# Late tiles transposed by DMA, W loads on GpSimd's queue, and new engine orders in a fused quantized attention and LoRA kernel

## The chip, the cores and the metric

One core of one Trainium2 chip runs the kernel. The metric is the device time of one execution in microseconds (us); the time of a version is the median of several runs.

## The reference, cut to what matters

```python
h   = x + tanh(g_xattn) * (q(layernorm(x)) @ q(ctx))        # q: round(x / s + z), clipped to 0..255, minus z, times s
y   = layernorm(h)
top = argmax(y @ gate_w.T + expert_bias)                    # one of 4 experts for each row
out = h + tanh(g_ffn) * (y @ W_up.T + lora_B[top] @ (lora_A[top] @ y))
```

`x` is 2 x 1024 x 2048 and each batch has its own `ctx` of 2048 x 2048; `W_up` is 2048 x 2048; the LoRA rank is 8. Everything comes and goes as float32.

## The kernel before, in words

The 2048 rows of x are 16 tiles of 128 rows (TILES); tiles 0 to 7 belong to the first batch. There are two stages, and TensorE goes from the one into the other.

**Stage 1** computes h. For each tile, VectorE takes the moments of the row (`moments`, L590 to L594), ScalarE a square root (`sqrt`, L374), VectorE the scale (`quant_scale`, L607), ScalarE rounds to int16 (`quant`, L380) and VectorE clips to bf16 (`clip`, L642). The clipped tile `q1` lies in `halves`, which has room for two tiles. TensorE transposes it in 16 blocks of 128 x 128 (`transposes`, L951 to L960) into two PSUM banks, and ScalarE copies them out to `rows_T` (`evac`, L399; for tiles 0 to 3 VectorE takes the second half, L654). `rows_T` holds four transposed tiles. Then come four chunks of 512 columns, 16 matmuls each (`part`, L969 to L988). VectorE adds each chunk to the row tile (`epi`, L649), and GpSimd's queue stores tiles 0 to 11 of h to HBM (L339) and loads the row tiles 6 to 15 of x (L335). The last four tiles of h stay in SBUF. Each chunk needs four of the 32 context tiles, which SP loads (L258), ScalarE rounds (`ctx_round`, L407) and VectorE clips (`ctx_clip`, L659). The four first tiles run interleaved, since the context arrives while they run: `stage1` (L993 to L1030) has that order written out. From tile 4 on the order is tile by tile, and the transposes of tile t+1 stand behind the first chunk of tile t.

**W** is 16 tiles of 128 x 2084 (`in_w`), brought in over three buffers: `normed`, `stage0` and `stage1`. SP issues all of them (`load_w`, L260 to L276). Loads 0 to 7 are W tiles 0 to 7, each taken through `abs_sum` (ScalarE, L416), `w_pow` (VectorE, L667 to L673), `w_high` (ScalarE, L425) and `w_low` (VectorE, L679); the buffer is free after `w_low`. Tiles 8 to 15 can't be stored before the second batch's context is done with, so they are loaded twice: loads 8 to 15 are for `abs_sum` alone, and loads 16 to 23 for `w_high` and `w_low`. Load i waits for the buffer's former user, and load 18 for `y_low(0)` as well. The common scale comes from `scales` on VectorE and an all-reduce on GpSimd (L359).

**Stage 2** computes y in two halves (high and low, f16) and multiplies by both halves of W in three products. `norm`, `y_high` and `y_low` (L633, L438, L687) make y; the first two tiles are transposed by TensorE (`y_transposes`, L1043) and scaled by VectorE (`yT_out`, L699), the others by one DMA transpose each from SP (L312). The first tile of stage 2 runs over the W tiles in order, five column blocks for each, for W tiles 0 to 10 (L1112 to L1119), and waits at each for `s_lo`, the count of `w_low`. It then waits for all 16 W tiles (L1121) and does the rest. Fifteen tiles of 240 matmuls each follow.

The orders of ScalarE (L463 to L547) and VectorE (L784 to L938) are written out by hand: `period(p, a, b, c)` interleaves the work of one tile with W or context work. An engine does its list strictly in order, and so does a DMA queue: a wait holds up all that stands behind it.

## Time and profile before

| what | value |
|---|---|
| median of 3 runs | 966.54 us (965.98 to 968.11) |
| the profiled execution's own time | 966.78 us |
| its span in the trace | 965.0 us |
| TensorE busy | 936.3 us, 97% |
| VectorE, ScalarE, GpSimd busy | 473.9, 233.8, 16.7 us |
| chain that ended last, TensorE's share | 93% |
| HBM read and written | 90.38 and 29.37 MB |

Times in the trace count from the first instruction. In the rows, PE is TensorE, DVE VectorE, ACT ScalarE, POOL GpSimd, and SP the engine that only issues DMAs. A matmul's length in a row includes its filling and draining; the pace is what the start times and the chain show.

### The profile page before, as it was taken

The page shows a single profiled execution, that of the slowest core. Times are in us where ns is not written, and L with a number is a line of the kernel's source. Part 1 is how long each engine was busy: PE and PEld are TensorE (multiplying, and loading weights), DVE is VectorE, ACT ScalarE, POOL GpSimd, SP SyncE. Part 2 cuts the span into 40 slices and gives each one's busy share as a digit, 9 for nine tenths or more (in the row PEclk, how much of TensorE's full clock was granted, in tenths as well). Part 3 has the DMA queues.
Part 4 walks back from the last instruction along what each step waited for, and adds up shares of the span by engine and source line. Part 5 has one row for each costly group of instructions (what it writes and reads, how often), then busy time and mean ns, then how long its engine had stood idle before and what let it go on. Part 6 is the DMA issues. An engine that isn't in the chain of part 4 may idle for free.

```text
span 965.0 us, 12440 instructions
## 1 busy us (share of the span) xinstructions
PE 936.3 (97%) x5239; PEld 500.9 (52%) x5264; DVE 473.9 (49%) x1023; ACT 233.8 (24%) x195; POOL 16.7 (2%) x40
## 2 busy tenths in 40 slices
PE   2899999999998999999999999999999999999998
PEld 1444444444455555555555555555555555555554
DVE  6695757785857526153443516253443516253421
ACT  5886777677622100000000000000000000000000
POOL 0001100010000000000000000000000000000000
PEclk9999999999999999999999999999999999999999
DMA  8999977678562232322222232222222132121211
GB/s 344 420 376 398 422 275 295 222 285 293 205 179 88 88 88 74 102 44 88 44 88 44 88 94 76 93 44 88 44 88 64 70 85 44 44 44 44 44 44 44
DMA packets 77082, 135.27 MB, mean 140 GB/s; under 512 B 61936, under 2 KB 62080, under 8 KB 62720
## 3 DMA queue, kind: packets, MB, share of 16 engines
q1 hardware_dynamic: 71088, 92.74, 29.4%
...
HBM read 90.38 MB, written 29.37 MB: 124 GB/s over the span
## 4 chain that ended last, share of the span: by engine, by line
PE 93%; DVE 3%; DMA 2%; ACT 1%; issue 1%; SPq 0%; ACTq 0%; DVEq 0%
PE bank L1051 67%; PE bank L981 23%; PE bank L958 2%; PE bank L1060 1%; DVE arena L679 1%; DMA normed<-in_w 1%; DMA rows<-in_x 1%; DVE bn L590 1%; ACT arena L425 0%; PE bank L1043 0%; ACT arena L407 0%; DVE halves L642 0%; DVE arena L659 0%; DVE normed L633 0%; SPq L280 0%
## 5 line engine op out<-in xcount | busy, mean ns | idle before, releaser
L1051 PE MATMUL bank<-arena,rows_T 128*128 128x416 f16 (+1 forms) x3840 | 685.2, 339 | 2.5 <-DVE arena L679 2.5
L1051 PEld LDWEIGHTS bank<-arena,rows_T 128*128 128x128 f16 x3840 | 373.0, 97 | 308.1 <-issue 4.8
L981 PE MATMUL bank<-arena,rows_T 128*128 128x512 bf16 x999 | 224.0, 382 | 4.5 <-DVE arena L659 2.7
L981 PEld LDWEIGHTS bank<-arena,rows_T 128*128 128x128 bf16 x1024 | 99.8, 98 | 122.1 <-issue 4.5
L773 DVE SCALAR_TENSOR_TENSOR rows<-bank,derived,rows 128x416 f32<-128x416 f32 (+2 forms) x80 | 49.9, 641 | 213.9 <-PE bank L1051 213.9
L446 ACT ACTIVATE z_stack_T<-bank 96x128 f16<-96x128 f16 x16 | 4.4, 272 | 556.0 <-PE bank L1066 556.0
L590 DVE BATCH_NORM_STATS2 bn<-rows 128x6 f32<-128x512 f32 x124 | 76.6, 679 | 3.7 <-DMA rows<-in_x 3.6
L713 DVE SCALAR_TENSOR_TENSOR route<-bank,derived,scal 128x4 f32<-128x4 f32 x16 | 3.5, 221 | 109.1 <-PE bank L1051 109.0
L649 DVE SCALAR_TENSOR_TENSOR rows<-bank,derived,rows 128x512 f32<-128x512 f32 x60 | 44.7, 748 | 22.6 <-PE bank L981 22.0
L781 DVE SCALAR_TENSOR_TENSOR rows<-bank,z_back_scale,rows 128x512 f32<-128x512 f32 x64 | 45.1, 746 | 10.6 <-PE bank L1060 6.6
L689 DVE SCALAR_TENSOR_TENSOR halves<-normed,ln,halves 128x2048 f16<-128x2048 f32 x14 | 32.9, 2351 | 29.0 <-ACT halves L440 29.0
L407 ACT ACTIVATE arena<-arena,scal,derived 128x2048 int16<-128x2048 f32 x22 | 44.9, 2083 | 0.8 <-DMA arena<-in_ctx 0.8
L440 ACT ACTIVATE halves<-normed,ln 128x2048 f16<-128x2048 f32 x14 | 28.0, 2002 | 48.3 <-DVE normed L637 48.3
L958 PE MATMUL bank<-ident_bf,halves 128*128 128x128 bf16 x256 | 18.7, 230 | 18.1 <-DVE halves L642 17.6
L380 ACT ACTIVATE halves<-rows,ln 128x2048 int16<-128x2048 f32 x15 | 31.4, 2091 | 9.0 <-DVE ln L614 9.0
L637 DVE SCALAR_TENSOR_TENSOR normed<-rows,ln,stage 128x2048 f32<-128x2048 f32 x14 | 32.9, 2352 | 0.5
L659 DVE TENSOR_SCALAR arena<-arena,derived 128x2048 bf16<-128x2048 int16 x32 | 23.8, 749 | 15.2 <-ACT arena L407 15.1
L679 DVE SCALAR_TENSOR_TENSOR arena<-stage,wscale,arena 128x2084 f16<-128x2084 f32 x11 | 26.1, 2383 | 9.9 <-ACT arena L425 9.8
L958 PEld LDWEIGHTS bank<-ident_bf,halves 128*128 128x128 bf16 x256 | 16.9, 104 | 22.5 <-issue 16.7
L399 ACT ACTIVATE rows_T<-bank 128x1024 bf16<-128x1024 bf16 x28 | 27.1, 1013 | 5.2 <-PE bank L958 5.2
L425 ACT ACTIVATE arena<-stage,wscale 128x2084 f16<-128x2084 f32 x11 | 22.1, 2027 | 22.4 <-DMA stage<-in_w 13.0
L599 DVE RECIPROCAL ln<-ln 128x1 f32<-128x1 f32 x32 | 5.1, 159 | 33.2 <-ACT ln L374 33.2
...
## 6 DMA issues: line engine op xcount, KB each, us to landing
arena<-in_ctx SPq DMA_DIRECT2D x22, 1024.0 KB, 15.7
stage<-in_w SPq DMA_DIRECT2D x17, 1042.0 KB, 5.5
out<-rows ACTq DMA_DIRECT2D x15, 1024.0 KB, 3.9
h_scratch<-rows POOLq DMA_DIRECT2D x11, 1024.0 KB, 7.6
rows<-h_scratch SPq DMA_DIRECT2D x11, 1024.0 KB, 4.8
stage<-in_ctx SPq DMA_DIRECT2D x10, 1024.0 KB, 8.5
rows<-in_x POOLq DMA_DIRECT2D x10, 1024.0 KB, 8.6
normed<-in_w SPq DMA_DIRECT2D x7, 1042.0 KB, 7.4
```

Of the source, the lines that this page charges most:

```text
L380: A(q1_i16(t), Xt(t), ACT.Relu, bias=L(t, "qb"), scale=L(t, "qs")).then_inc(s_qi, 1)
L407: A(Qc(c, True), buf, ACT.Relu, bias=z2, scale=V["rs2"]).then_inc(s_cr, 1)
L590: v.bn_stats(bn[:, u % 2, i, :], Xc(u, i * 512, (i + 1) * 512)).then_inc(s_bn, 1)
L637: v.scalar_tensor_tensor(out=T[:, 0:D], in0=Xt(u), scalar=L(u, "mean"), in1=WR, op0=ALU.subtract, op1=ALU.mult).then_inc(s_norm, 1)
L649: v.scalar_tensor_tensor(out=xs, in0=bank[ROT[g % 6]][:, :], scalar=V["coef"], in1=xs, op0=ALU.mult, op1=ALU.add).then_inc(s_epi, 1)
L679: v.scalar_tensor_tensor(out=W(n, 1), in0=wbuf[k][:, :], scalar=wa[:, n:n + 1], in1=W(n, 0), op0=ALU.mult, op1=ALU.subtract).then_inc(s_lo, 1)
L689: v.scalar_tensor_tensor(out=HL[:, 1, :], in0=T[:, 0:D], scalar=L(TILES + s, "rstd"), in1=HL[:, 0, :], op0=ALU.mult, op1=ALU.subtract).the ...
L773: v.scalar_tensor_tensor(out=xs, in0=bank[c][:, a - CUT[c]:b - CUT[c]], scalar=V["gs"], in1=xs, op0=ALU.mult, op1=ALU.add).then_inc(s_e2, 1)
L781: v.scalar_tensor_tensor(out=xs, in0=TR[j % 2], scalar=gl[:, s % 2:s % 2 + 1], in1=xs, op0=ALU.mult, op1=ALU.add).then_inc(s_el, 1)
L958: mm = nc.tensor.transpose(TR[g].bitcast(BF16)[:, i * P:(i + 1) * P], q1(t)[:, k * P:(k + 1) * P], idb[:, :])
L981: mm = mmul(bk, q1T[:, t % 4, kt, :], Q(b, n, kt), start=(kt == 0), stop=(kt == KT - 1 and not slow), skip_group_check=True)
L1051: mm = mmul(bank[c][:, 0:b - a], YT[:, s % 2, yh, kt, :], W(kt, wh, a, b), start=(first and kt == kts[0] and yh == 0 and wh == 0), stop=(k ...
```

## The change

Tiles 9 to 15 of `q1` are transposed by DMA from SP into `rows_T` (`q1_transpose`) instead of by TensorE and ScalarE; two semaphores, for even and odd tiles, count them, and `by_dma` waits for them. SP also gets the row tiles 11 to 15, the stores of tiles 7 to 11, the load of `b_t` and the small LoRA loads. All 24 W loads go to GpSimd's queue, behind its last row load and store, with the all-reduce between loads 17 and 18. From tile 8 on ScalarE and VectorE have a new order, written out item by item; around the start of stage 2, `w_low(9)` to `w_low(11)` stand earlier. At the start of the kernel the orders of all engines change too: row tile 2 is loaded ahead of context tile 1, tiles 1 and 2 are rounded and transposed earlier, and TensorE gets 6 and 8 products of zeros (384 columns each, on the zeroed `d1`, into a bank that is overwritten) around the transposes of tile 0. The diff is without the semaphores' declarations and the context lines; the body of `load_w` is as at L260 to L276, with pool for sp.

```diff
+    BY_DMA = 9
+    BY_SP = 7
...
+    BY_V = [(1, 0), (2, 1), (3, 1)]
...
-by_pool = [u for u in range(SPARE + 1, TILES)] + [TILES + KEEP]
+by_pool = [u for u in range(SPARE + 1, BY_SP + 4)]
...
-        return s_hg[slot(u)], count(u, range(TILES - KEEP))
+        if u < BY_SP:
+            return s_hg[slot(u)], count(u, range(BY_SP))
+        return s_h[slot(u)], count(u, range(BY_SP, TILES - KEEP))
...
+def by_dma(engine, t):
+    engine.wait_ge(s_xt[t % 2], 16 * ((t - BY_DMA) // 2 + 1))
...
-        if u >= TILES:
+        if u > SPARE:
...
-    def load_w(i):
...
+    def q1_transpose(t):
+        sp.wait_ge(s_q1, t + 1)
+        sp.wait_ge(s_mm, place[(t - 4, NCH - 1)] + 1)
+        sp.dma_start_transpose(q1T[:, t % 4], q1(t)).then_inc(s_xt[t % 2], 16)
+    def store(t):
+        sp.wait_ge(s_epi, place[(t, NCH - 1)] + 1)
+        sp.dma_start(h_t[t], Xt(t)).then_inc(s_h[slot(t)], 16)
...
+    row(2)
...
-    row(2)
-    for c in range(2, 6):
-        ctx_tile(c)
+    ctx_tile(2)
+    ctx_tile(3)
...
+    ctx_tile(4)
+    ctx_tile(5)
...
-    for i in range(KT + 8):
-        load_w(i)
+    row(11)
+    store(7)
+    q1_transpose(9)
+    row(12)
+    q1_transpose(10)
+    q1_transpose(11)
+    store(8)
+    row(13)
+    store(9)
+    q1_transpose(12)
+    row(14)
+    store(10)
+    q1_transpose(13)
+    store(11)
+    row(15)
+    q1_transpose(14)
+    q1_transpose(15)
+    sp.wait_ge(*stored(former(TILES + KEEP)))
+    sp.dma_start(Braw, b_t).then_inc(s_braw, 16)
...
+    sp.wait_ge(s_bp, 2)
+    sp.dma_start(brow_d, bp[0:E * R, 1:2]).then_inc(s_br0, 16)
+    sp.wait_ge(s_br0, 16)
+    sp.dma_start(br[:, :], brow_d.rearrange("k o -> (k o)").unsqueeze(0).to_broadcast(
+        [P, E * R])).then_inc(s_br, 16)
...
+    sp.wait_ge(s_bst, 1)
+    row(TILES + KEEP)
...
+    nc.gpsimd.memset(d1[:, :, :], 0.0).then_inc(s_pool, 1)
...
-    pool.wait_ge(s_pool, 2)
+    pool.wait_ge(s_pool, 3)
...
-    nc.gpsimd.memset(d1[:, :, :], 0.0).then_inc(s_id, 1)
...
-        if u >= TILES:
-            pool.wait_ge(*stored(u - TILES - KEEP))
-            src = h_t[u - TILES - KEEP]
-        else:
-            src = x_t[u]
-        nc.gpsimd.dma_start(Xt(u), src).then_inc(s_xg[slot(u)], 16)
+        nc.gpsimd.dma_start(Xt(u), x_t[u]).then_inc(s_xg[slot(u)], 16)
...
-    for t in range(7, TILES - KEEP):
-        store(t)
-        row(t + 4)
-    pool.wait_ge(*stored(former(TILES + KEEP)))
-    nc.gpsimd.dma_start(Braw, b_t).then_inc(s_braw, 16)
+    def load_w(i):
+        n, k = W_LOADS[i]
...
+        if i == KT + 2:
+            pool.wait_ge(s_yl, 1)
+        nc.gpsimd.dma_start(wbuf[k][:, :], w_t[n]).then_inc(s_w[k], 16)
+    for i in range(KT + 2):
+        load_w(i)
...
-    pool.wait_ge(s_bp, 2)
-    nc.gpsimd.dma_start(brow_d, bp[0:E * R, 1:2]).then_inc(s_br0, 16)
-    pool.wait_ge(s_br0, 16)
-    nc.gpsimd.dma_start(br[:, :], brow_d.rearrange("k o -> (k o)").unsqueeze(0).to_broadcast(
-        [P, E * R])).then_inc(s_br, 16)
-    pool.wait_ge(s_bst, 1)
-    row(TILES + KEEP)
+    for i in range(KT + 2, KT + 8):
+        load_w(i)
...
-        if t >= 2:
+        if t >= BY_DMA + 2:
+            by_dma(act, t - 2)
+        elif t >= 2:
...
-            if t >= 1:
+            if t > BY_DMA:
+                by_dma(act, t - 1)
+            elif t >= 1:
...
+    def half(t, g):
+        act.wait_ge(s_tr, 2 * t + g + 1)
+        if t >= 4:
+            act.wait_ge(s_mm, place[(t - 4, NCH - 1)] + 1)
+        A(q1T[:, t % 4, GROUP * g:GROUP * (g + 1), :].rearrange("p k m -> p (k m)"),
+          TR[g].bitcast(BF16), ACT.Copy).then_inc(s_ev, 1)
...
-        for g in range(1 if t < HEAD else 2):
-            act.wait_ge(s_tr, 2 * t + g + 1)
-            if t >= 4:
-                act.wait_ge(s_mm, place[(t - 4, NCH - 1)] + 1)
-            A(q1T[:, t % 4, GROUP * g:GROUP * (g + 1), :].rearrange("p k m -> p (k m)"),
-              TR[g].bitcast(BF16), ACT.Copy).then_inc(s_ev, 1)
+        half(t, 0)
+        half(t, 1)
...
-            act.wait_ge(s_tr, 2 * TILES)
+            by_dma(act, TILES - 2)
+            by_dma(act, TILES - 1)
...
+    sqrt(1)
...
-    sqrt(1)
-    evac(0)
+    half(0, 0)
+    quant(1)
+    half(0, 1)
+    sqrt(2)
...
-    quant(1)
+    quant(2)
+    half(1, 1)
...
-    sqrt(2)
-    evac(1)
-    quant(2)
+    half(2, 0)
...
-    evac(2)
+    sqrt(3)
...
-    sqrt(3)
+    quant(3)
...
-    quant(3)
...
-    evac(3)
+    half(3, 0)
...
-        evac(p + 1)
+        if p + 1 < BY_DMA:
+            evac(p + 1)
...
-    period(8, lambda: abs_sum(0), lambda: w_high(0), lambda: abs_sum(1))
-    for p in range(9, 12):
-        n = 2 * p - 17
-        period(p, lambda: (w_high(n), abs_sum(n + 1)), lambda: w_high(n + 1), lambda: abs_sum(n + 2))
-    period(12, lambda: (w_high(7), abs_sum(8)), lambda: abs_sum(9), lambda: abs_sum(10))
-    period(13, lambda: abs_sum(11), lambda: abs_sum(12), lambda: abs_sum(13))
-    period(14, lambda: abs_sum(14), lambda: (sqrt(TILES), abs_sum(15)), lambda: y_high(0))
+    abs_sum(0)
+    sqrt(10)
+    w_high(0)
+    abs_sum(1)
+    quant(10)
+    abs_sum(2)
+    w_high(1)
+    sqrt(11)
+    quant(11)
+    sqrt(12)
+    abs_sum(3)
+    w_high(2)
+    abs_sum(4)
+    quant(12)
+    w_high(3)
+    abs_sum(5)
+    w_high(4)
+    w_high(5)
+    abs_sum(6)
+    sqrt(13)
+    w_high(6)
+    quant(13)
+    abs_sum(7)
+    w_high(7)
+    sqrt(14)
+    abs_sum(8)
+    abs_sum(9)
+    quant(14)
+    abs_sum(10)
+    sqrt(15)
+    abs_sum(11)
+    quant(15)
+    abs_sum(12)
+    abs_sum(13)
+    abs_sum(14)
+    sqrt(16)
+    abs_sum(15)
+    y_high(0)
...
-    for n in range(8, 14):
+    for n in range(8, KT - 1):
...
-    for n in range(14, KT):
-        w_high(n)
+    w_high(KT - 1)
...
-        dve.wait_ge(s_id, 2 + E)
+        dve.wait_ge(s_pool, 3)
+        dve.wait_ge(s_id, 1 + E)
...
-    def moments(u):
+    def moments(u, first=0, end=4):
...
-        for i in range(4):
+        for i in range(first, end):
...
-            elif i == 3 or u > 0:
+            elif i in (3, first):
...
+        if end < 4:
+            return
...
-    def evac_second(t):
-        dve.wait_ge(s_tr, 2 * t + 2)
-        v.tensor_copy(q1T[:, t % 4, GROUP:2 * GROUP, :].rearrange("p k m -> p (k m)"),
-                      TR[1].bitcast(BF16)).then_inc(s_evb, 1)
+    def half(t, g):
+        dve.wait_ge(s_tr, 2 * t + g + 1)
+        v.tensor_copy(q1T[:, t % 4, GROUP * g:GROUP * (g + 1), :].rearrange("p k m -> p (k m)"),
+                      TR[g].bitcast(BF16)).then_inc(s_tv, 1)
...
+    def scalars():
+        dve.wait_ge(s_tanh, 2)
+        step(v.tensor_tensor(V["coef"], s1, s2, ALU.mult))
+        step(v.tensor_tensor(V["coef"], V["coef"], V["tx"], ALU.mult))
+        step(v.tensor_scalar(V["cd"], V["coef"], V["dl2"], -1.0, ALU.mult, ALU.mult))
+        step(v.tensor_scalar(V["ce"], V["cd"], V["dl1"], -float(D), ALU.mult, ALU.mult))
...
+    scalars()
...
-    dve.wait_ge(s_tanh, 2)
-    step(v.tensor_tensor(V["coef"], s1, s2, ALU.mult))
-    step(v.tensor_tensor(V["coef"], V["coef"], V["tx"], ALU.mult))
-    step(v.tensor_scalar(V["cd"], V["coef"], V["dl2"], -1.0, ALU.mult, ALU.mult))
-    step(v.tensor_scalar(V["ce"], V["cd"], V["dl1"], -float(D), ALU.mult, ALU.mult))
...
-    ctx_clip(0)
...
-    evac_second(0)
-    ctx_clip(1)
...
+    quant_scale(2)
+    ctx_clip(0)
+    ctx_clip(1)
+    clip(2)
+    half(1, 0)
+    moments(3, 0, 2)
...
-    quant_scale(2)
-    evac_second(1)
-    clip(2)
+    half(2, 1)
...
-    evac_second(2)
+    moments(3, 2, 4)
+    quant_scale(3)
...
-    moments(3)
...
+    ctx_clip(6)
+    clip(3)
...
-    quant_scale(3)
-    ctx_clip(6)
+    ctx_clip(7)
+    delta_parts()
...
-    ctx_clip(7)
+    ctx_clip(8)
...
-    clip(3)
-    evac_second(3)
+    half(3, 1)
...
+    ctx_clip(9)
...
+    ctx_clip(10)
...
-    ctx_clip(8)
-    ctx_clip(9)
-    ctx_clip(10)
-    delta_parts()
...
-    period(8, lambda: w_pow(0), nothing, lambda: (w_low(0), w_pow(1)))
-    for p in range(9, 12):
-        n = 2 * p - 17
-        period(p, lambda: w_low(n - 1) if n > 1 else None, lambda: (w_low(n), w_pow(n + 1)), lambda: w_pow(n + 2))
-    period(12, lambda: w_low(6), lambda: w_low(7), nothing)
-    period(13, nothing, nothing, nothing)
...
-    period(14, lambda: moments(TILES), lambda: norm(0), scales)
+    epi(7, 3)
+    moments(10)
+    w_pow(0)
+    quant_scale(10)
+    w_low(0)
+    w_pow(1)
+    clip(10)
+    moments(11)
+    quant_scale(11)
+    epi(8, 0)
+    w_low(1)
+    clip(11)
+    epi(8, 1)
+    moments(12)
+    w_pow(2)
+    epi(8, 2)
+    epi(8, 3)
+    epi(9, 0)
+    w_pow(3)
+    epi(9, 1)
+    quant_scale(12)
+    epi(9, 2)
+    w_low(2)
+    w_low(3)
+    clip(12)
+    epi(9, 3)
+    epi(10, 0)
+    epi(10, 1)
+    w_pow(4)
+    epi(10, 2)
+    w_pow(5)
+    moments(13)
+    w_low(4)
+    epi(10, 3)
+    w_low(5)
+    epi(11, 0)
+    w_pow(6)
+    quant_scale(13)
+    epi(11, 1)
+    w_low(6)
+    epi(11, 2)
+    clip(13)
+    epi(11, 3)
+    epi(12, 0)
+    moments(14)
+    w_pow(7)
+    w_low(7)
+    epi(12, 1)
+    epi(12, 2)
+    quant_scale(14)
+    clip(14)
+    moments(15)
+    epi(12, 3)
+    quant_scale(15)
+    epi(13, 0)
+    epi(13, 1)
+    epi(13, 2)
+    clip(15)
+    epi(13, 3)
+    moments(16)
+    epi(14, 0)
+    norm(0)
+    epi(14, 1)
+    epi(14, 2)
+    scales()
...
+    w_low(9)
...
+    epi(15, 3)
+    w_low(10)
+    w_low(11)
...
-    epi(15, 3)
...
-    for n in range(9, 14):
-        w_low(n)
+    w_low(12)
+    w_low(13)
...
-        if g and t < HEAD:
-            pe.wait_ge(s_evb, t + 1)
+        if t >= BY_DMA:
+            by_dma(pe, t)
+        elif (t, g) in BY_V:
+            pe.wait_ge(s_tv, BY_V.index((t, g)) + 1)
...
-            pe.wait_ge(s_ev, t + 1 if t < HEAD else HEAD + 2 * (t - HEAD) + g + 1)
+            pe.wait_ge(s_ev, 2 * t + g + 1 - sum(1 for h in BY_V if h < (t, g)))
+    def zeros(n):
+        for i in range(n):
+            mmul(bank[0][:, 0:3 * P], d1[:, 0, :], d1[:, :, :].rearrange("p a b -> p (a b)"), start=True,
+                 stop=True)
...
+        pe.wait_ge(s_pool, 1)
+        pe.wait_ge(s_ve, 1)
+        zeros(6)
...
+        zeros(8)
+        transposes(1)
...
-        transposes(1)
+        transposes(2)
...
-        transposes(2)
+        part(0, 0, 3, 4, slow)
...
-        for t in range(LEAD):
-            part(t, 0, 3, 4, slow)
-        for k in range(3):
-            for t in range(LEAD):
-                part(t, 1, k, k + 1, slow)
-        transposes(LEAD)
-        for t in range(LEAD):
-            part(t, 1, 3, 4, slow)
+        part(2, 1, 0, 1, slow)
+        part(1, 0, 3, 4, slow)
+        part(2, 1, 1, 2, slow)
+        part(1, 1, 0, 1, slow)
+        part(0, 1, 0, 1, slow)
+        part(0, 1, 1, 2, slow)
+        part(2, 1, 2, 3, slow)
+        part(2, 0, 3, 4, slow)
+        part(1, 1, 1, 2, slow)
+        transposes(3)
+        part(1, 1, 2, 3, slow)
+        part(0, 1, 2, 3, slow)
+        part(0, 1, 3, 4, slow)
+        part(1, 1, 3, 4, slow)
+        part(2, 1, 3, 4, slow)
...
-                if n == 0 and t + 1 < TILES:
+                if n == 0 and t + 1 < BY_DMA:
...
-            half_out(TILES - 1, g)
+            half_out(BY_DMA - 1, g)
```

## Rows read from the trace of the kernel before

**Rows 1.** The page: busy time, share of the span and instructions of each engine

```profile
PE 936.3 (97%) x5239; PEld 500.9 (52%) x5264; DVE 473.9 (49%) x1023; ACT 233.8 (24%) x195; POOL 16.7 (2%) x40
```

**Rows 2.** TensorE in order of time, 0 to 120 us: start, length, instructions

```profile
16.04 0.80 PE L958 MATMUL bank<-ident_bf,halves 128*128 128x128 bf16 x6 [16.04 <-DVE halves L642]
...
25.12 1.89 PE L958 MATMUL bank<-ident_bf,halves 128*128 128x128 bf16 x16 [1.58 <-DVE halves L642]
...
34.35 12.90 PE L981 MATMUL bank<-arena,rows_T 128*128 128x512 bf16 x58 [1.40 <-DVE arena L659]
```

**Rows 3.** The chain that ended last, in order of time: start, length, what

```profile
207.27 0.89 PE bank L958 x16
...
221.98 0.89 PE bank L958 x16
...
292.79 2.39 DVE arena L679
...
303.33 5.29 PE bank L1051 x30
```

**Rows 4.** TensorE in order of time, 215 to 330 us

```profile
254.68 1.50 PE L1043 MATMUL bank<-ident_h,halves 128*128 128x128 f16 x24
...
263.54 29.25 PE L1051 MATMUL bank<-arena,rows_T 128*128 128x416 f16 x165
295.32 7.12 PE L1051 MATMUL bank<-arena,rows_T 128*128 128x416 f16 x30 [2.53 <-DVE arena L679]
```

**Rows 5.** Windows, TensorE alone: stretch, length, busy (instructions), granted clock, DMA share, GB/s

```profile
296.00:297.00 1.00, 1.00 (x5) 0.50 0.85 287
```

**Rows 6.** ScalarE in order of time, 0 to 320 us

```profile
17.75 1.02 ACT L399 ACTIVATE rows_T<-bank 128x1024 bf16<-128x1024 bf16 x1 [1.84 <-PE bank L958]
...
215.74 2.09 ACT L380 ACTIVATE halves<-rows,ln 128x2048 int16<-128x2048 f32 x1 [1.79 <-DVE ln L614]
...
275.75 2.03 ACT L425 ACTIVATE arena<-stage,wscale 128x2084 f16<-128x2084 f32 x1 [10.94 <-DMA stage<-in_w]
```

**Rows 7.** VectorE in order of time, 130 to 330 us

```profile
160.63 2.46 DVE L590 BATCH_NORM_STATS2 bn<-rows 128x6 f32<-128x512 f32 x4
...
208.65 2.46 DVE L590 BATCH_NORM_STATS2 bn<-rows 128x6 f32<-128x512 f32 x4
...
218.58 0.75 DVE L642 TENSOR_SCALAR halves<-halves,derived 128x2048 bf16<-128x2048 int16 x1
...
251.57 2.28 DVE L687 TENSOR_TENSOR halves<-normed,halves 128x2048 f16<-128x2048 f32 x1
...
265.10 2.38 DVE L679 SCALAR_TENSOR_TENSOR arena<-stage,wscale,arena 128x2084 f16<-128x2084 f32 x1
```

**Rows 8.** DMA issues, 130 to 250 us: engine, count, size, us to landing

```profile
stage<-in_w SPq DMA_DIRECT2D x13, 1042.0 KB, 5.5
h_scratch<-rows POOLq DMA_DIRECT2D x6, 1024.0 KB, 5.8
```

**Rows 9.** VectorE in order of time, 0 to 130 us

```profile
11.38 2.47 DVE L590 BATCH_NORM_STATS2 bn<-rows 128x6 f32<-128x512 f32 x4 [0.58 <-DMA rows<-in_x]
...
15.14 0.75 DVE L642 TENSOR_SCALAR halves<-halves,derived 128x2048 bf16<-128x2048 int16 x1
```

**Rows 10.** The instructions on rows_T that SP issues: DMA transposes

```profile
L312 SPq DMA_TRANSPOSE rows_T<-halves x14: 4731/4832/5502, 338.6 to 900.2; - x14
...
DMA to landing us min/median/max: 6.7/6.7/8.3
```

**Rows 11.** DMA queues, 338 to 347 us: packets, MB, share of the stretch

```profile
q1 hardware_dynamic: 4128, 1.05, 70.3%
```

**Rows 12.** DMA in 40 slices of 2 us, 160 to 240 us: GB/s

```profile
GB/s 208 370 426 381 197 63 333 138 4 393 266 398 416 167 333 150 0 393 250 422 413 167 325 154 0 393 279 398 438 304 243 388 408 408 434 400 292 271 0 38
```

**Rows 13.** Windows, all engines: busy, granted clock, DMA share, GB/s

```profile
189.09:203.79 14.70, 14.60 (x80) 7.17 (x80) 12.06 (x26) 10.61 (x11) 1.07 (x2) 1.00 0.71 268
```

**Rows 14.** What SP issues, in order of time, 0 to 420 us

```profile
142.60 0.80 SPq L276 DMA_DIRECT2D stage<-in_w  x2
```

More of the change, by code:

```diff
@@ L173, in build @@
         s_xg = [sem(f"row_tile_loaded_by_pool{i}") for i in range(XB)]
+        s_h = [sem(f"late_h_tile_stored{i}") for i in range(XB + 1)]
         s_hg = [sem(f"h_tile_stored{i}") for i in range(XB + 1)]
@@ L184, in build @@
         s_tr = sem("transposed"); s_ev = sem("transposes_out")
-        s_evb = sem("second_half_out")
+        s_tv = sem("transposes_out_by_vector")
         s_mm = sem("chunk_done"); s_epi = sem("chunk_out")
@@ L192, in build @@
         s_wc = sem("w_back_scale"); s_wr0 = sem("w_back_row_parked"); s_wr = sem("w_back_row_loaded")
-        s_dt = sem("y_transposed_by_dma")
+        s_xt = [sem(f"q1_transposed_by_dma{i}") for i in range(2)]; s_dt = sem("y_transposed_by_dma")
         s_m2 = sem("chunk2_done"); s_dl = sem("delta_done"); s_rt = sem("route_step"); s_zs = sem("z_stack_ready"); s_gl = sem("z_back_scale_ready")
@@ L352, in _ @@
             store(6)
[L353 to L357 removed]
+            def load_w(i):
+                n, k = W_LOADS[i]
+                before = [j for j in range(i) if W_LOADS[j][1] == k]
+                if not before:
+                    if k:
+                        pool.wait_ge(s_cr, CT)
+                    else:
+                        pool.wait_ge(*stored(SPARE))
+                if before:
+                    j = before[-1]
+                    if HALF <= j < KT:
+                        pool.wait_ge(s_sum, j + 1)
+                    else:
+                        pool.wait_ge(s_lo, j + 1 if j < HALF else j - HALF + 1)
+                if i == KT + 2:
[3 more added lines that the diff above has]
+                load_w(i)
             pool.wait_ge(s_pm, 1)
             nc.gpsimd.partition_all_reduce(V["PM"], V["pm"], P, bass.bass_isa.ReduceOp.max).then_inc(s_PM, 1)
[L360 to L366 removed]
+            for i in range(KT + 2, KT + 8):
+                load_w(i)
         @block.scalar
```

16 lines of the change are left out of this document (removed).

## The prediction

> **What bounds the kernel now.** I read the page first: TensorE is busy for 97% of the span [rows 1], so only work taken off TensorE, or a wait of it that ends earlier, can shorten the run. The chain of waits in order of time shows which. From 34.35 to 263.54 us it runs on TensorE without a wait: blocks of 16 transposes (L958, 0.89 us) and of matmuls, one block of transposes in each tile of 14.71 us (221.98 - 207.27) [rows 2 to 4]. VectorE and ScalarE lie beside it. TensorE loses time in two places. The first is the head: it starts at 16.04, and its matmuls have no wait left only from 34.35 on; 16 transposes there take 1.89 us in place of 0.89 [rows 2, 3], so TensorE ran at about half pace, the lower of its two levels (1.2 of 2.4 GHz). The second is the start of stage 2: 165 matmuls from 263.54, then a wait of 2.53 us for the last `w_low`, then 30 matmuls in 7.12 us where the same 30 later take 5.29; the granted clock is 0.50 in between [rows 3 to 5]. Stage 2 behind that is TensorE work that the change doesn't touch.
>
> **The change, part by part**, against the profiled execution (966.78 us, span 965.0; 0.24 above the median).
>
> **Transposes off TensorE.** Tiles 9 to 15 lose a block each: 7 x 0.89 = 6.2 us, all on the path [rows 3]. ScalarE loses 14 copies of about 1 us [rows 6], which were beside the path; they give it room.
>
> **Start of stage 2.** In the old list `w_low(9)` stands behind two epilogues, two `yT_out` and `b_scale`, and starts at 265.10 [rows 7]; load 20 (W tile 12) can be issued only when it ends, at 267.5, and its user on ScalarE starts at 275.75 after 10.94 us of waiting [rows 6]. In the new list `w_low(9)` goes ahead of about 4.3 us of that work, and 10 and 11 ahead of the two `yT_out`. Count from the first product of stage 2. `w_low(9)` ends near 0 (now +3.9), load 20 lands 5.5 later [rows 8]; `w_low(10)` and `(11)` end by +5.5; two `yT_out`, `b_scale` and `w_low(12)` take 2.4 + 0.6 + 2.4, to +10.9; load 23 lands at +16.4, and after `y_high(1)` (2.1), `w_high(15)` (2.0) and `w_low(15)` (2.4) all W is ready at about +23. TensorE asks for it at +29.3 (292.79 - 263.54) [rows 3, 4]. So the wait of 2.53 goes, and the low clock behind it (7.12 - 5.29 = 1.8): 4.4 us. With 6 us of slack even the late landing of now doesn't bring it back. Bounds: 0 and 4.4.
>
> **The W loads' queue.** In the same stretch a store from GpSimd lands 5.8 us after its issue and a W load from SP 5.5 [rows 8]. I take 0.3 us a load, hidden; bounds 0 and 1. Load 0 now waits behind `store(6)`, about 1 us, before the context is done, with no user yet. The all-reduce stands ahead of load 18, which waits for `y_low(0)` anyway. The small LoRA loads go to SP; `route(0)` needs them only after W is ready, 20 us after `b_scale`. These I cost at nothing.
>
> **Head.** `clip(0)` waits for the scalars behind `moments(1)`; ahead of them it starts some 0.8 us earlier, when `moments(1)` is through [rows 9]. The transposes of tile 1 start at 25.12 now. In the new list ScalarE does, from the moments' end at 14.3, `sqrt(1)` 0.2, `ctx_round(0)` 2.0, a copy 0.9 and `quant(1)` 2.0, VectorE a clip 0.7: 20.2. Up to 34.35 the old list did three blocks of transposes and 24 matmuls; from about 22 the new one has one block and these 24 left, 6.1 us at full clock. If the clock stays low until 30, as now, that ends near 32.2, which is 2.1 us of gain. Against it stands that context tiles come at their old pace, so part is waited away. I take 1.4; bounds 0 and 2.5. The products of zeros cost nothing while TensorE waits for `clip(0)` and `clip(1)`: 8 x 0.35 us at the low clock (384 columns, three times the 0.12 us of a transpose there, 1.89 / 16) end before 20.2. What they may do is raise the clock earlier. The Trainium skill (TensorE: Matmul & The Clock Gate, "What's actually happening") says that activity is what releases the throttle; by that the zeros might bring the upper bound, 2.5, in place of 1.4. The slow matmuls of the head and the 0.50 after the wait agree with it [rows 2, 5].
>
> **New waits of TensorE.** A DMA transpose of 1 MB occupies SP's issue for 4.8 us and lands after 6.7 [rows 10]; a tile of q1 is half of that: 2.4 us of all queues' time and 6.7 - 2.4 = 4.3 to landing when nothing is ahead. The upper bound is half the queues' share of that stretch, 0.703 x 9 / 2 = 3.2 us [rows 11]. It now needs a place among the W loads, at 2.5 us each (1.04 MB near 410 GB/s, what full slices move) [rows 12], and the DMA queues are already at 0.71 in such a tile [rows 13]. When TensorE wants a tile follows from the grid: a chunk takes (14.71 - 0.89) / 4 = 3.46 us, so after the block at 221.98 (tile 14's, behind the first chunk of tile 13) tile 14 begins at 221.98 + 0.89 + 3 x 3.46 = 233.2, tile 9 at 159.7 and tile 8 at 145.0. The tiles with the least room:
> - Tile 9 stands on SP behind `row(11)` and `store(7)`, which can go when tile 7 is done, 145.0 - 1.4 + 0.8 = 144.4. Loads 1 and 2, now at 142.60 [rows 14], come at the same time. Three transfers ahead: 144.4 + 7.5 + 4.3 = 156.2. TensorE wants it at 159.7 - 1.4 - 0.9 = 157.4. It holds, with 1.2 us to spare.
> - Tile 14: `quant(14)` is at 215.74 and its clip ends at 219.3 now [rows 6, 7]. TensorE wants it at 233.2 - 1.4 - 6 x 0.89 = 226.5. With one W load ahead it lands at 219.3 + 2.5 + 4.3 = 226.1, with two at 228.6. Loads 10 to 13 come together here, so I take two: 2.2 us.
> - `y_low(0)` ends at 253.85 and TensorE wants it at 254.68 [rows 4, 7]; now it is wanted 7.6 us earlier. It hangs on the W loads through `abs_sum(15)`. The new order is to speed this; I take 0.3.
> Together +2.5; bounds 0 (each lands in time) and 8.
>
> The sum: -6.2 - 4.4 - 1.4 + 2.5 = -9.5, so 966.78 - 9.5 = 957.3, and 957.0 on the scale of the median.
>
> **The rivals.**
> - *Transposes starve behind the W loads* (chance 0.15). 1.05 MB go in 4128 packets, some 254 bytes each [rows 11], and a row of W is 8.3 KB. If the two queues take turns packet by packet, a transpose gets almost nothing until GpSimd's queue is empty. Tile 14 then waits for all of loads 10 to 12, 219.3 + 7.5 + 4.3 = 231.1, 4.7 us late, and the low clock follows as after the 2.53 us of now (1.8): waits of 6.5 + 0.3 in place of 2.5, 961.3. For it speaks the packet size; against it, that no row shows the two together. The Trainium skill (DMA: Bandwidth & Descriptors, "Queues, rings and completion order") says that a DMA engine goes round its queues one packet at a time, though it counts several descriptors to a packet; the trace can't show here which it is.
> - *VectorE and the W work still set the pace* (0.12). From 160.63 to 208.65 the moments come every 16.0 us, not every 14.7: VectorE lags, and catches up only behind tile 13 [rows 7]. It is busy for 12.1 of 14.7 us there [rows 13], so the lag is waiting, not work. If the new order keeps it, `y_low(0)` is as late as 253.85 less the head's 1.4 and TensorE waits 5.4 us more: 962.4.
> - *The DMA queues fill up, and it gets slower* (0.09). Between 142.6 and 238 they must move W loads 1 to 17, five row tiles and five stores at 2.5 us each, `b_t` at 1.9, and seven transposes: 67.5 + 1.9 + 16.8 = 86 of 95 us. Let a transpose of 0.5 MB hold them as long as one of 1 MB does (4.8): 103 us. The overrun of 8 us comes once at tile 9, through late rows and W tiles, and again before `y_low(0)`, where now nothing is spare; with the clock's 1.8 each time, 12 to 16 us of waits against 12 of gain: 968. It decides from a price of about 4.5 us for a transpose (an overrun of 6 us, twice). Against it stands half the bytes and half the packets.
> - *The waits are nil and the head takes its upper bound* (0.12): 966.54 - 6.2 - 4.4 - 2.5 = 953.4.
>
> **How the numbers follow.** The forecast has 0.52. The range runs from 953.5 to 963.5: it holds the forecast, the first two rivals and most of the last. What a measurement of this kernel can tell from no change is about 0.2%, 1.9 us. Faster by more than that are all cases but the third rival, and a little of the second: 0.88. Within it 0.03, slower 0.09.
>
> **What would show it.** In the changed kernel: no L958-like blocks after tile 8 and a tile of 13.8 us; the transposes of tile 1 near 20; 165 matmuls at the start of stage 2 with no wait for W behind them and a clock of 1.00; and waits of TensorE for the transposes on `rows_T` at tile 14, some 2 us. The forecast is wrong if tile 9 waits too, or if the transposes land more than 10 us after their issue; then the DMA rivals hold.

## The result, and the profile after

| version | median | runs | ratio to before, 95% interval |
|---|---|---|---|
| before, run beside it | 965.91 us | 8 (963.98 to 968.11) | |
| after | 972.88 us | 8 (968.05 to 980.48) | 1.0079 [1.0051, 1.0108] |

The change makes the kernel slower, by 7 us, where 9.5 us of gain were forecast; the time lies outside the range. It also spreads more from run to run, over 12 us in place of 4. The profiled execution took 972.03 us.

The page of the kernel after: span, busy times, and two DMA queues (packets, MB, share of the span); q1 carries what SP issues, q0 what GpSimd issues.

```profile
span 970.0 us, 12227 instructions
...
PE 932.9 (96%) x5143; PEld 495.8 (51%) x5166; DVE 472.5 (49%) x1022; ACT 221.7 (23%) x182; POOL 23.3 (2%) x50
...
q1 hardware_dynamic: 84080, 83.14, 28.6%
q0 software_dynamic: 5184, 38.19, 11.9%
```

Against [rows 1], TensorE does less and the span is still 5.0 us longer. The waits of TensorE, in us, times and longest, say where it went:

```profile
PE bank L1130 <- DMA rows_T<-halves: 13.1, 2, 10.5
PE bank L1097 <- DVE derived L867: 11.6, 1, 11.6
PE bank L1107 <- DVE halves L720: 2.5, 2, 1.7
PE bank L1212 <- DVE arena L757: 2.4, 1, 2.4
```

L1097 and L1107 are the head. The first line is new: two waits, 13.1 us, for DMA transposes. The last is the old wait for the last `w_low` (L757, formerly L679), which was to go. TensorE in order of time shows both in place, 10 to 310 us:

```profile
20.53 1.89 PE L1107 MATMUL bank<-ident_bf,halves 128*128 128x128 bf16 x16 [0.72 <-DVE halves L720]
...
159.09 69.23 PE L1130 MATMUL bank<-arena,rows_T 128*128 128x512 bf16 x314 [2.65 <-DMA rows_T<-halves]
...
238.78 22.66 PE L1130 MATMUL bank<-arena,rows_T 128*128 128x512 bf16 x94 [10.46 <-DMA rows_T<-halves]
261.28 1.50 PE L1204 MATMUL bank<-ident_h,halves 128*128 128x128 f16 x24
...
270.14 29.25 PE L1212 MATMUL bank<-arena,rows_T 128*128 128x416 f16 x165
301.81 5.43 PE L1212 MATMUL bank<-arena,rows_T 128*128 128x416 f16 x30 [2.42 <-DVE arena L757]
```

The waits at 159.09 and 238.78 are for tiles 9 and 14. The 94 matmuls from 238.78 take 22.66 us; the same 94 take 20.88 in another run below, so the low clock after the wait (granted 0.50 from 239 to 242 us) costs 1.8. Stage 2 starts at 270.14, in place of 263.54 [rows 4]. The 30 matmuls at 301.81 have a wait of 2.42 ahead of them, nearly as before, but run in 5.43 and not in 7.12.

The chain that ended last, in order of time: start, length, what.

```profile
143.96 15.00 DMA rows_T<-halves
...
218.41 20.24 DMA rows_T<-halves
...
264.68 14.86 DMA stage<-in_w
...
289.54 7.60 DMA stage<-in_w
```

So a transpose of half a megabyte took 15.0 and 20.2 us from issue to landing, where one of a whole megabyte took 6.7 [rows 10], and a W load just before stage 2 took 14.9, where in stage 1 before they took 5.5 [rows 8] and at the start of stage 2 up to 10.0. The instructions on `rows_T` that SP issues, tiles 9 to 15 (duration in ns of the issue, minimum, median, maximum):

```profile
L275 SPq DMA_TRANSPOSE rows_T<-halves x7: 4727/7609/9526, 144.0 to 226.4; - x7
...
DMA to landing us min/median/max: 7.9/9.7/20.2
```

What the queues did is in the DMA view of three stretches (packets, MB, share of the stretch). From 218 to 222 us, with tile 14's transpose issued at 218.41:

```profile
DMA packets 216, 1.64 MB, mean 411 GB/s; under 512 B 19, under 2 KB 19, under 8 KB 19
...
q0 software_dynamic: 216, 1.64, 102.5%
```

from 222 to 226 us:

```profile
DMA packets 1884, 1.00 MB, mean 251 GB/s; under 512 B 1819, under 2 KB 1819, under 8 KB 1819
...
q0 software_dynamic: 81, 0.54, 126.7%
q1 hardware_dynamic: 1803, 0.46, 57.6%
```

and from 226 to 238 us:

```profile
DMA packets 1112, 2.17 MB, mean 181 GB/s; under 512 B 877, under 2 KB 877, under 8 KB 877
...
q1 hardware_dynamic: 846, 0.21, 48.1%
q0 software_dynamic: 266, 1.96, 39.9%
```

First GpSimd's queue has all of the engines, and the transpose gets nothing. Then 1803 of its packets go in 4 us; half of a whole megabyte's 4128 [rows 11] would be 2064, so little of tile 14 is left. But GpSimd has issued W loads at 220.88 and 223.69, SP issues tile 15's transpose at 226.41, and from 226 on everything crawls: 2.17 MB and 846 small packets in 12 us. W loads alone move 1.64 MB in 4, and transposes alone 4128 packets in 9 [rows 11]; at these two paces what went in the 12 us would have taken some 4.8 + 1.8 = 6.6 (an estimate). Tile 14 lands at 238.65, as the last of the two loads does.

### The profile page after: what moved, and what is told of

It reads as the page before. It is cut to its first block, busy times and chain, and to the rows that moved or that the text cites. A ratio compares the mean times of both kernels' runs of the same rounds, so it can differ in the third digit from the quotient of the medians.

```text
span 970.0 us, 12227 instructions
## 1 busy us (share of the span) xinstructions
PE 932.9 (96%) x5143; PEld 495.8 (51%) x5166; DVE 472.5 (49%) x1022; ACT 221.7 (23%) x182; POOL 23.3 (2%) x50
## 4 chain that ended last, share of the span: by engine, by line
PE 86%; DMA 7%; DVE 3%; ACT 2%; issue 1%; SPq 0%; POOL 0%; DVEq 0%; ACTq 0%; POOLq 0%
PE bank L1212 67%; PE bank L1130 17%; DMA rows_T<-halves 4%; DMA stage<-in_w 2%; PE bank L1221 1%; DMA rows<-in_x 1%; DVE arena L757 1%; ACT arena L449 1%; DVE bn L666 1%; ACT halves L417 1%; PE bank L1107 1%; ACT arena L467 0%; ACT rows_T L437 0%; DVE rows L727 0%; DVE halves L765 0%
## 5 line engine op out<-in xcount | busy, mean ns | idle before, releaser
L1130 PE MATMUL bank<-arena,rows_T 128*128 128x512 bf16 x1001 | 223.5, 382 | 15.9 <-DMA rows_T<-halves 13.1
L757 DVE SCALAR_TENSOR_TENSOR arena<-stage,wscale,arena 128x2084 f16<-128x2084 f32 x11 | 26.2, 2382 | 12.6 <-ACT arena L467 12.5
L449 ACT ACTIVATE arena<-stage,scal,derived 128x2048 int16<-128x2048 f32 x10 | 20.6, 2084 | 0.1
L1221 PE MATMUL bank<-stage,z_stack_T 96*128 96x512 f16 x64 | 19.1, 379 | 0.0
L1097 PE MATMUL bank<-delta_parts 128*128 128x384 bf16 x14 | 4.8, 522 | 11.6 <-DVE derived L867 11.6
## 6 DMA issues: line engine op xcount, KB each, us to landing
h_scratch<-rows POOLq DMA_DIRECT2D x6, 1024.0 KB, 13.1
```

The costliest lines, as they stand in the source:

```text
L449: A(Qc(c, True), buf, ACT.Relu, bias=z2, scale=V["rs2"]).then_inc(s_cr, 1)
L757: v.scalar_tensor_tensor(out=W(n, 1), in0=wbuf[k][:, :], scalar=wa[:, n:n + 1], in1=W(n, 0), op0=ALU.mult, op1=ALU.subtract).then_inc(s_lo, 1)
L1130: mm = mmul(bk, q1T[:, t % 4, kt, :], Q(b, n, kt), start=(kt == 0), stop=(kt == KT - 1 and not slow), skip_group_check=True)
L1221: mmul(TR[j % 2], zT[:, :], Bst[:, j * NB:(j + 1) * NB], start=True, stop=True).then_inc(s_dl, 1)
```

## The experiments

Line numbers in a fence are those of its own kernel. In SP's and GpSimd's lists a W load is `load_w(i)`. Each ratio is to the kernel before on the same chip, whose medians lie between 964.85 and 967.25 us (10 to 22 runs). So where two experiments ran beside different runs of before, their medians compare only to about 2 us; where that matters the difference of the ratios, times 966 us, stands beside.

| run | what | median (range, runs) | ratio, 95% interval |
|---|---|---|---|
| a_late_small | small transfers later | 976.21 (973.66 to 977.96, 4) | 1.0091 [1.0065, 1.0117] |
| b_hold | three W loads held for transposes | 978.64 (975.06 to 982.02, 4) | 1.0118 [1.0082, 1.0154] |
| c_one_queue | all W loads in SP's queue | 955.16 (954.51 to 955.73, 4) | 0.9876 [0.9858, 0.9893] |
| d_tensore | transposes on TensorE | 966.78 (964.69 to 969.62, 10) | 0.9998 [0.9986, 1.0010] |
| e_small_last | small transfers last | 972.87 (965.52 to 976.24, 10) | 1.0063 [1.0037, 1.0089] |
| g_tensore_one_queue | c, transposes on TensorE | 959.91 (959.55 to 961.32, 7) | 0.9941 [0.9922, 0.9959] |
| h_head | before, new head alone | 963.57 (962.37 to 965.87, 10) | 0.9981 [0.9966, 0.9997] |
| i_no_zeros | c without zero products | 954.79 (954.26 to 959.13, 5) | 0.9887 [0.9871, 0.9904] |
| j_early_small | c, wback's transfer early | 956.78 (956.64 to 957.69, 4) | 0.9912 [0.9882, 0.9942] |
| k2_five_on_gpsimd | c, five W loads on GpSimd | 965.73 (956.36 to 973.65, 10) | 0.9995 [0.9965, 1.0026] |
| l_quarter_loads | e, each W load in four parts | 976.36 (973.60 to 977.05, 4) | 1.0102 [1.0082, 1.0122] |
| m_five_on_scalar | c, five W loads on ScalarE's queue | 976.44 (968.53 to 977.53, 7) | 1.0104 [1.0075, 1.0132] |

**The four corners: where the transposes are done, and in how many queues.** c moves all W loads from GpSimd's queue into SP's list, between the rows, stores and transposes, and the small transfers behind the last W load. d takes the kernel after and gives the transposes back to TensorE, and their copies to ScalarE. g does the same to c.

```diff
c_one_queue: SP's list (GpSimd's has none of them left)
+load_w(0)  row(11)  +load_w(1)  +load_w(2)  store(7)  q1_transpose(9)  +load_w(3)
 row(12)  q1_transpose(10)  q1_transpose(11)  +load_w(4)  store(8)  row(13)  +load_w(5)  +load_w(6)
 store(9)  q1_transpose(12)  row(14)  +load_w(7)  store(10)  +load_w(8)  +load_w(9)  q1_transpose(13)
 store(11)  row(15)  +load_w(10)  +load_w(11)  +load_w(12)  q1_transpose(14)  +load_w(13)  +load_w(14)
 q1_transpose(15)  +load_w(15)  Braw  +load_w(16) to +load_w(23)  small transfers
d_tensore and g_tensore_one_queue
-BY_DMA = 9
+BY_DMA = 16
-q1_transpose(9) ... q1_transpose(15)
+evac(9) ... evac(15)
```

> The changed kernel with all W loads back on SP, in one list with the row loads, stores and DMA transposes, in the order in which they were issued in the profile; the small transfers stand behind the last W load. Only the queue is changed, not the bytes. Theory of starvation by the second queue: in one queue a transpose waits only for what stands ahead of it; tiles 9 and 14 land within 12 us, TensorE waits 0 to 3 us for them, the wait at the start of stage 2 is gone, and the time is 957 to 963. Rival of full queues: landings of the transposes stay at 13 to 20 us and the time at 968 to 974.

> The changed kernel with tiles 9 to 15 transposed by TensorE again and copied out by ScalarE; the rest (queues, orders, head, small transfers) as changed. This prices the DMA transposes alone. TensorE gets 7 x 0.89 = 6.2 us of work back and loses the waits of 13.1 us and the low clock of some 1.9 behind them: 972.9 + 6.2 - 15.0 = 964 (961.5 to 966.5) if the orders around the copies fit. Rival, that the new orders and GpSimd's queue cost time by themselves: 968 to 973.

> The version with one queue, which measured 955.2, with tiles 9 to 15 transposed by TensorE and copied out by ScalarE again. This prices the DMA transposes where nothing starves them. Theory: they are worth the seven blocks of 0.89 us, 6.2 us, and nothing else: 961.4 (960 to 963), and no wait at the start of stage 2. Rival, that one queue alone made the gain and the DMA transposes are worth nothing: 955 to 957.

Measured: 972.9 with the transposes by DMA beside W loads in another queue, 955.2 with the same transposes in one queue with them; on TensorE 966.8 and 959.9. (c came out below its expected range, d 0.3 above its own, g within.) So the DMA transposes cost 6.1 us with two queues (7.8 by the ratios) and gain 4.8 with one (6.3). In c's trace only one wait for a transpose is left, TensorE in order of time, 120 to 310 us:

```profile
132.17 1.06 PE L1121 MATMUL bank<-ident_bf,halves 128*128 128x128 bf16 x16
...
157.74 89.95 PE L1144 MATMUL bank<-arena,rows_T 128*128 128x512 bf16 x408 [0.34 <-DMA rows_T<-halves]
...
256.38 34.53 PE L1226 MATMUL bank<-arena,rows_T 128*128 128x416 f16 x195
```

and its transposes land in time; SP's instructions on `rows_T` and the DMA view of 217 to 245 us:

```profile
L293 SPq DMA_TRANSPOSE rows_T<-halves x7: 1822/5996/9027, 144.9 to 225.1; - x7
...
DMA to landing us min/median/max: 4.4/9.2/12.7
...
DMA packets 5227, 8.88 MB, mean 317 GB/s; under 512 B 4287, under 2 KB 4287, under 8 KB 4287
...
q1 hardware_dynamic: 5224, 8.85, 103.9%
```

The median landing of 9.2 us hardly differs from that of after (9.7), since W loads stand ahead in the list; it is the longest that went from 20.2 to 12.7. The start of stage 2 is one stretch of 195 matmuls: both the wait for `w_low` and the low clock are gone. In d they aren't, and weigh more as TensorE comes there earlier:

```profile
262.45 29.25 PE L1211 MATMUL bank<-arena,rows_T 128*128 128x416 f16 x165
296.56 7.45 PE L1211 MATMUL bank<-arena,rows_T 128*128 128x416 f16 x30 [4.86 <-DVE arena L756]
```

4.86 and 7.45 - 5.43 = 2.0 of low clock are 6.9 us, and d comes to stage 2 later than g by 262.45 - 261.37 = 1.1: together they are the 7.9 us between the two spans (966.5 and 958.6). The medians differ by 6.9 (5.5 by the ratios). So much is the one queue, with the small transfers last, worth while the transposes are on TensorE; with them by DMA it is worth 17.7 (972.9 - 955.2; 19.6 by the ratios).

**Which second queue.** k2 takes c and issues W loads 10 to 14 alone from GpSimd; m issues the same five from ScalarE, whose queue is a hardware queue like SP's.

```diff
k2_five_on_gpsimd, on c_one_queue (m_five_on_scalar: the same, issued by ScalarE behind abs_sum(8) to abs_sum(11))
-sp: load_w(10) ... load_w(14)
+pool: for i in range(10, 15): load_w(i)
```

> The version with one queue (955.2), with W loads 10 to 14 alone on GpSimd's queue; they are the five that are in flight around the DMA transposes of tiles 14 and 15. Theory of starvation by the second queue: tile 9 lands as in one queue (within 13 us, TensorE waits 0 to 1 us), and tiles 14 and 15 land 15 to 20 us after their issue; TensorE waits 7 to 12 us for tile 14, and the low clock may follow: 963 to 969. Rival, that the effect comes from all loads being behind GpSimd's work or from its issue time: tile 14 lands as in one queue, and the time is 955 to 957.

> One queue for all W loads and transposes gave 955.2 us; with W loads 10 to 14 on GpSimd's queue the same order gave 965.7, spread from 956 to 974. Here the same five loads are issued from ScalarE's own hardware queue instead, behind abs_sum(8) to abs_sum(11). Theory that any second queue beside the transposes slows them: about 966, with a spread of some 15 us, and transposes of tiles 12 to 14 that land after 12 us and more. Rival, that it is only GpSimd's software queue: 955 to 957, spread under 3 us, with the transposes landing in 4 to 13 us as in one queue.

Five loads of 24 are enough: k2 spread from 956.36 to 973.65 us, where the four of c lie within 1.2, and m took 976.44, 21 us more than c. Without its two longest (970.87 and 973.65) the median of k2 is 963.94, still 8.8 more than c. So it isn't only GpSimd's software queue: the other hardware queue does it too. Nor does m's order hold the transpose back: SP issues that of tile 14 at 216.92, in c at 217.05. The profiled execution of k2 was one of the short ones (956.36), with TensorE in order of time

```profile
227.84 20.88 PE L1161 MATMUL bank<-arena,rows_T 128*128 128x512 bf16 x94 [1.61 <-DMA rows_T<-halves]
```

while m's has the largest wait of the case:

```profile
241.24 22.58 PE L1164 MATMUL bank<-arena,rows_T 128*128 128x512 bf16 x96 [15.36 <-DMA rows_T<-halves]
```

and the DMA view of m, 226 to 240 us, what went on ahead of it (q1 is SP's queue, q10 ScalarE's):

```profile
DMA packets 1414, 2.00 MB, mean 143 GB/s; under 512 B 1209, under 2 KB 1209, under 8 KB 1209
...
q1 hardware_dynamic: 1181, 0.29, 72.1%
q10 hardware_dynamic: 233, 1.71, 44.0%
```

The engines are booked to 116% and move 143 GB/s; in one queue c moved 317 over a stretch with two transposes in it. But the two queues don't always meet like this. In k2's short execution they are side by side as well, 222 to 232 us, and tile 14 lands after 11.4 us, where in m it took 24.2 (q0 is GpSimd's queue):

```profile
DMA packets 3482, 3.13 MB, mean 313 GB/s; under 512 B 3202, under 2 KB 3202, under 8 KB 3202
...
q0 software_dynamic: 328, 2.33, 64.4%
q1 hardware_dynamic: 3154, 0.80, 45.8%
```

**Holding loads back.** b keeps two queues, but three W loads wait until the transposes that they would meet have landed.

```diff
+AFTER_T = {1: 9, 13: 14, 15: 15}
+if i in AFTER_T:
+    by_dma(pool, AFTER_T[i])
```

> The changed kernel with W loads 1, 13 and 15 held back until the DMA transposes of tiles 9, 14 and 15 have landed. Theory: a transpose goes out in pieces of 256 bytes and gets one turn for each 8.3 KB piece of W, so it starves while GpSimd's queue has W loads. Held back, the transposes of tiles 9 and 14 land in 5 to 9 us after issue in place of 15 and 20, TensorE waits for them 0 to 4 us in place of 13.1, and the time is 961 to 966. Rival, that the DMA queues are simply full in this stretch: the wait moves from the transposes to the W loads and to y_low(0), and the time stays at 969 to 975. The small transfers still delay W at the start of stage 2 in both.

The transposes did land sooner (4.3/8.6/13.1 us), and TensorE waited for none of them. But the W loads and all behind them came later, load 1 at 151.21 instead of 140.62, and TensorE waits 4.89 us for rows, 7.45 for `y_low(0)` and 5.31 for the last `w_low` instead: 978.6, the slowest of all, and above both expected ranges. The W chain has no slack that a wait may use up; order within one queue costs none, as c shows.

**Cutting the loads.** If the queues take turns piece by piece, the size of W's pieces against the transposes' 256 bytes sets how they share. l cuts each load in four by columns, on the base of e. A row's part is then 2.1 KB, but the queue's packets are of 4.2 KB in place of 8.3 (5.4 MB in 1290 packets over 2 KB, 264 to 290 us), so what is tested is half the size, not a quarter.

```diff
-dma_start(wbuf[k][:, :], w_t[n])
+for q in range(4): dma_start(wbuf[k][:, a:b], w_t[n][:, a:b])
```

> The changed kernel with the small transfers last (972.9), with each W load cut into four transfers of 521 columns, so that a piece of W is 2.1 KB and not 8.3 KB; same bytes, same queue. Theory that the queues take turns piece by piece: a transpose's 256 bytes then wait for a quarter of what they waited for, tiles 9 and 14 land after 9 to 14 us in place of 15 to 20, TensorE waits for them 3 to 8 us in place of 16, and the time is 961 to 967. Rival, that the second queue is simply served first, or that both are slowed whatever the size: landings of 15 to 20 us and 970 to 975.

976.4, and TensorE waits 15.1 us for transposes, in four places, with landings of 8.4/12.5/17.4 us; in e it waits 16.4, with landings of 6.3/13.5/19.8. Packets of half the size helped the time nothing, which speaks against a turn by pieces as the whole account; a quarter wasn't tried.

**The small transfers.** `wback` goes to HBM in 2048 pieces of 4 bytes. In the kernel before SP issues it at 280.61, behind all W loads; in the kernel after at 261.54, ahead of the last five. a holds it and the LoRA transfers until `w_low` 13; e until the last W load has landed; j takes c and puts it ahead of load 19.

```diff
a_late_small   +sp.wait_ge(s_lo, 13)                     ahead of both
e_small_last   +sp.wait_ge(s_w[1], w_loaded(KT + 7))     ahead of both, LoRA's first
j_early_small  (c)  load_w(16) to load_w(18), wback's transfer, load_w(19) to load_w(23)
```

> The changed kernel (972.9) with one wait more: SP issues the small transfer of wback (2048 pieces of 4 bytes), and the two LoRA ones behind it, only when w_low has done 13 tiles, that is when the last W load is out. Theory: the small pieces written to HBM hold up the W loads at the start of stage 2 (the load issued at 264.68 landed 14.9 us later). Then W loads 19 to 23 land within 4.5 to 7 us, the wait of 2.4 us after the 165 matmuls goes, and the time is 970.5 (968.5 to 971.5). Rival: the long landing comes from GpSimd's queue itself; then the loads still take 8 to 15 us and the time stays at 972 to 974. The DMA transposes in stage 1 are as they were in both.

> The changed kernel with the small transfers (wback to HBM in 2048 pieces of 4 bytes, and the two LoRA ones) issued only when the last W load has landed. In the run before this one they went out in the same moment as that load, and W was no earlier. Theory: writing small pieces to HBM holds up every W load in flight beside them. Then loads 19 to 23 land in 4.5 to 7 us each, W is ready before TensorE wants it, and the wait at the start of stage 2 (2.4 to 3.9 us) is gone: 970 (967.5 to 971.5), with the waits for tiles 9 and 14 as they were. Rival, GpSimd's queue is slow by itself: loads 19 to 23 stay at 8 to 15 us, and so does the wait; 972 to 975.

> The version with one queue (955.2), with the transfer of wback in 2048 pieces of 4 bytes moved ahead of W load 19, where the changed kernel has it in time. Theory: the small pieces hold up the W load behind them by about 10 us, in one queue as in two; W is ready 8 to 10 us later, and TensorE waits 1 to 4 us for it: 957 to 962. Rival: only two queues side by side make the delay; then load 19 lands within 7 us and the time stays at 955 to 956.

W loads between 255 and 310 us land in 5.2/10.1/14.9 us in the kernel after; in e they do in

```profile
L395 POOL DMA_DIRECT2D stage<-in_w x5: 530/535/540, 256.2 to 288.2; - x5
L395 POOL DMA_DIRECT2D normed<-in_w x2: 530/634/737, 268.0 to 280.7; - x2
...
DMA to landing us min/median/max: 5.1/5.2/5.5
```

and no wait for `w_low` is left in e. In a one load was still issued in the same instant as the small transfers and landed after 17.4 us: a wait of 3.93, where its expectation had none (a took 976.2, not 970.5; the transposes cost it 13.8). j has landings of up to 14.2 where c has 5.3, a wait of 1.52 at the start of stage 2 and 1.6 us more in its median (3.5 by the ratios). So the small transfers hold up the W loads behind them, which the prediction left out. In the kernel before it seems to be the same: its loads issued at 267.5, 269.8 and 272.1 land after 8.2, 9.8 and 10.0 us, long before `wback`'s transfer, but beside the LoRA ones, which GpSimd issues at 265.20 (32 pieces of 4 bytes) and 271.72. The DMA view of before, 268 to 273 us:

```profile
DMA packets 73, 0.61 MB, mean 122 GB/s; under 512 B 0, under 2 KB 0, under 8 KB 0
...
q1 hardware_dynamic: 73, 0.61, 89.9%
```

The engines are booked to 90% and move 122 GB/s. No run moved the LoRA transfers alone, so this stays a likely reading.

But e's total hardly moved, as its trace drew waits of 6.41 and 10.03 us for tiles 9 and 14: with two queues, the transposes decide.

**The head.** h has the new start, and nothing else, on the kernel before; i is c without the 14 products of zeros.

> The kernel before with the new start alone: order of row and context tiles, of ScalarE, VectorE and TensorE up to the third chunk, and the 14 products of zeros. TensorE reached the transposes of tile 8 2.4 us earlier in the changed kernel (131.2 in place of 133.6). Theory: that is the start's worth, and it stays to the end, since the W chain is long enough behind: 964.5 (963.5 to 965.5) against 967. Rival: the W loads and VectorE's chain set the start of stage 2, the wait there grows by what the start gains, and the time is 966 to 967.5.

> The version with one queue (955.2) without the 14 products of zeros at the start. Theory: they raise TensorE's clock a few us earlier, since otherwise it idles before and between the first transposes; without them the first matmuls run at half pace until about 30 us, and the time is 955.5 to 957. Rival: the context tiles set the pace of the start anyway, and nothing changes: 955.0 to 955.4.

h is 2.1 us below before (1.8 by the ratio). In the traces, the transposes of tile 8 start at 133.57 before,

```profile
131.21 1.06 PE L1107 MATMUL bank<-ident_bf,halves 128*128 128x128 bf16 x16
```

in the kernel after, at 130.75 in h, 132.17 in c and 130.76 in i. The zeros bring nothing that can be measured: 954.8 without them, 955.2 with them (0.9887 and 0.9876). Nor do they bring full pace sooner. In i, without them, TensorE in order of time shows

```profile
20.08 1.89 PE L1121 MATMUL bank<-ident_bf,halves 128*128 128x128 bf16 x16 [3.29 <-DVE halves L734]
...
25.74 1.05 PE L1121 MATMUL bank<-ident_bf,halves 128*128 128x128 bf16 x16
...
249.68 1.60 PE L1216 MATMUL bank<-ident_h,halves 128*128 128x128 f16 x24 [3.90 <-DVE halves L779]
```

and in c the same blocks take 1.89 at 21.65 and 1.05 at 27.14. The granted clock reads 1.00 throughout the head, before and in i, so the slow pace there is read from lengths alone. The last line is a wait for `y_low(0)` that c doesn't have: the profiled execution of i is its longest (959.13; the other four took 954.3 to 955.0), and it gives back there more than its start had gained.

## Why the prediction was wrong

**The step that failed is "The W loads' queue", and with it "New waits of TensorE".** The move to GpSimd's queue was priced as 0.3 us a load, hidden, and the transposes as waiting for their place among the W loads: 2.2 us for tile 14, and tile 9 in time. They wait for a place only within one queue. In two, the trace shows 15.0 us for tile 9 (156.2 - 144.4 = 11.8 were counted) and 20.2 for tile 14 (9.3 counted), a cost of 13.1 us and 1.8 of low clock; c, with the same transposes, the same loads and the same orders of the other engines, pays 0.34. Of the signs that the prediction named, the wait for tile 9 came. The other, landings of more than 10 us after the issue, came too but was badly chosen: the prediction's own count for tile 9 is 11.8, and c, where almost nothing is waited for, has landings of up to 12.7.

**The rivals.** The nearest is the first, starving behind the W loads. Its first half is what 218 to 222 us shows: nothing of the transpose moves until the loads ahead of it are through. It then let the transpose land in 4.3 us, and so gave 961.3. And 1803 packets did go by 226 us. But loads 13 and 14 were in flight by then, and with them the rest crawled to 238.65; that is how tile 14 alone came to cost 10.5 us. The rule that I set beside it (the Trainium skill, DMA: Bandwidth & Descriptors, "Queues, rings and completion order": turns by packet) doesn't foresee that the sum of both slows; 181 and 143 GB/s against 411 do show it, and l, at half the size, gives no sign that the pieces are the lever. The same page of the Trainium skill, under "Issuing engines are not separate DMA queues", says that issuing from several engines saves only the time to issue; here the choice of queue for five loads is worth 21 to 22 us (m against c, by medians and by ratios), and the measurement decides. The third rival had the sign, for another reason: the queues don't fill, since in c the transposes' issues hold SP for 6.0 us at the median, over the 4.5 from which that rival was to decide, and almost nothing is late.

**Start of stage 2, -4.4.** Right in its order of work: in c, e and g, where nothing holds up the loads, the wait and the low clock are both gone. Wrong in the kernel after, because of a transfer that the sum has no term for: the new lists let `wback`'s go ahead of the last five loads, and neither the W loads' paragraph nor its "These I cost at nothing" names it. W loads that were to land in 5.5 us took up to 14.9, and 2.42 us of wait stay. Only the 1.8 of clock is gained. The late landing of before, against which the prediction left 6 us of slack, most likely came of the LoRA transfers.

**Transposes off TensorE, -6.2.** Right. From the transposes of tile 8 to the first product of stage 2, c takes 256.38 - 132.17 = 124.2 us and g 261.37 - 131.40 = 130.0; with c's 0.34 of wait taken out, 6.1 for seven blocks.

**Head, -1.4.** 2.4 in the trace of after, 1.4 in c, 2.8 in h and in i: within or just over the bounds of 0 and 2.5. The transposes of tile 1 start at 20.53, where 20.2 was counted. The prediction laid the upper bound to the zeros, by the Trainium skill (TensorE: Matmul & The Clock Gate, "What's actually happening"), for which activity releases the throttle; without the zeros it comes as well, so here that reason falls.

**The sum again**, on spans, with what was measured: 965.0 - 6.2 - 2.4 + 13.1 + 1.8 - 1.8 - (2.53 - 2.42) = 969.4, against 970.0. For c: 965.0 - 6.2 - 1.4 - 4.3 + 0.34 = 953.4, against 953.7. The forecast of 957.0 was in effect one for c, which took 955.2: 1.2% below before and 1.8% below after.

**Not settled:** why the two kinds slow each other, and why only in some meetings. No run had two queues of loads beside a transpose that was smaller or in larger packets, and none had a transpose beside stores alone. Why one execution of k2 takes 956 us and another 974 isn't shown either; the profiled one is of the short ones, and I suppose that it depends on which transfers happen to meet.
